# A four-layer graph network on one core: untransposed first weights, a table copy in pieces, larger rings, and layer 2's own rows added by an identity product

## What is computed

```
f0: w = relu(edge_attr @ W1.T + b1) @ W2.T + b2;  agg = segment_sum(w * x[src], dst)
    relu(x @ Ws.T + bs + agg @ Wn.T + bn)
f1: 10 times  out = 0.9 * segment_sum(w * out[col], row) + 0.1 * h;   out / theta
f2: 16 times  h = 0.9 * segment_sum(norm * h[row], col) + 0.1 * x     (self-loops added, norm from degrees)
f3: twice     h = prelu(segment_sum(norm * (h @ W)[src], dst) + b)    (self-loops added)
```

## Time and profile before

| | |
|---|---|
| runs (3) | 9433.23, 9444.26, 9446.84 us; median 9444.26 |
| profiled execution | 9456.96 us, its span 9455.1 us |
| busy: PE / PEld / DVE / ACT / POOL | 44% / 34% / 55% / 23% / 73% of the span |
| 0 to 323 us | histograms |
| 330 to 349 us | node_records |
| 355 to 988 us | rank_edges |
| 989 to 1318 us | prepare |
| 1323 to 4135 us | layer 1, 10 passes |
| 4135 to 8659 us | layer 2: own rows gathered and split until 4383, then 16 passes |
| 8659 to 9455 us | layer 3 |

### The profile page before, as it was taken

One profiled execution on the slowest core, in us unless ns is written; L12 is line 12 of the kernel. 1 busy time (PEld: TensorE's weight loads), 2 busy tenths in 40 slices (PEclk: granted clock), 3 DMA queues, 4 the chain that ended last, 5 costly groups with the idle time before them and its releaser, 6 DMA issues. The chain is left out here.

```text
span 9455.1 us, 78421 instructions
## 1 busy us (share of the span) xinstructions
PE 4182.3 (44%) x18929; PEld 3224.8 (34%) x18929; DVE 5165.0 (55%) x12775; ACT 2149.3 (23%) x5789; POOL 6906.2 (73%) x7074
## 2 busy tenths in 40 slices
PE   6566654444344443311444444444444443333643
PEld 5455542232222332211333333333333332223643
DVE  6566654454444445643555656555555665465454
ACT  1266542111011110331211111111111110036433
POOL 5565567777777777767777777777777777777777
PEclk9666665555555555555555555555555555555555
DMA  7755253333333333432444444433333343333311
GB/s 116 126 160 176 83 97 98 101 102 97 97 96 97 102 102 97 109 87 67 109 108 109 111 111 107 107 107 103 104 103 103 106 107 95 93 95 86 91 46 38
DMA packets 924098, 957.38 MB, mean 101 GB/s; under 512 B 385766, under 2 KB 814140, under 8 KB 923546
## 3 DMA queue, kind: packets, MB, share of 16 engines
q1 hardware_dynamic: 652470, 588.49, 20.8%
q0 software_dynamic: 225792, 323.35, 17.4%
q10 hardware_dynamic: 45382, 40.53, 1.3%
HBM read 561.02 MB, written 418.54 MB: 104 GB/s over the span
## 5 line engine op out<-in xcount | busy, mean ns | idle before, releaser
L1803 POOL DMA_INDIRECT l_g<-tab,l x2940 | 2889.3, 983 | 906.8 <-issue 852.7
L1972 DVE TENSOR_TENSOR_SCAN l_w<-l_m,l_w,bank 96x512 f32<-96x512 bf16 x1248 | 1591.9, 1276 | 2619.8 <-PE bank L1830 2613.1
L1830 PE MATMUL bank<-ident,l_g 128*96 128x128 f32 x5096 | 1334.0, 415 | 3309.6 <-DMA l_g<-tab,l 1706.0
L1830 PEld LDWEIGHTS bank<-ident,l_g 128*96 128x96 f32 x5096 | 843.3, 187 | 3905.8 <-DMA l_g<-tab,l 1877.3
L1803 POOL DMA_INDIRECT l_g<-tab,XM x1764 | 1731.0, 981 | 549.5 <-issue 514.9
L1841 PE MATMUL bank<-ident,l_w 96*128 96x96 f32 x5096 | 1055.3, 359 | 77.7 <-DVE l_w L1972 76.8
L1841 PEld LDWEIGHTS bank<-ident,l_w 96*128 96x128 f32 x5096 | 938.9, 227 | 121.0 <-DVE l_w L1972 108.3
L352 ACT ACTIVATE tail_sc<-tail_mv,eps_x 125x4 f32<-125x4 f32 (+1 forms) x149 | 44.3, 297 | 3511.5 <-DVE tail_mean L344 3416.0
L288 PE MATMUL bank<-tail_up,v 96*96 96x500 f32 (+1 forms) x298 | 296.4, 1098 | 437.5 <-DVE tail_up L279 437.5
L2016 DVE TENSOR_TENSOR l_o<-l_o,coef_d 128x384 f32<-128x384 f32 x735 | 411.9, 560 | 25.4
L2025 DVE TENSOR_TENSOR T<-l_o,XM 128x384 f32<-128x384 f32 x735 | 405.3, 555 | 0.0
(11 more groups left out here) (301 smaller groups left out, 9291.3 us busy)
## 6 DMA issues: line engine op xcount, KB each, us to landing
tab<-l_o SPq DMA_DIRECT2D x1176, 192.0 KB, 2.4
l_m<-mask_d SPq DMA_DIRECT2D x784, 96.0 KB, 2.7
l_m<-mask_s SPq DMA_DIRECT2D x490, 96.0 KB, 2.7
l_g<-tab,l POOLq DMA_INDIRECT x2940
l_g<-tab,XM POOLq DMA_INDIRECT x1764
x3t<-XM SPq DMA_DIRECT2D x98, 192.0 KB
x_meta<-in_x_dram SPq DMA_DIRECT2D x25, 750.0 KB
x1t<-XM ACTq DMA_DIRECT2D x100, 187.5 KB
```

The source lines that it names most:

```text
L1803: nc.gpsimd.indirect_dma_start(out=tile(G[q % RG], t), out_offset=None, in_=tables[0:table_at + (2 - p % 2) * TR, :] if p else first, in_o ...
L1830: last = nc.tensor.transpose(a_bank(q)[0:D, u:GE:U], G[q % RG][:, u * D:(u + 1) * D], self.ident[:, :])
L1972: v.tensor_tensor_scan(out=W[q % RW][:, :], data0=masks[q % RM][:, :], data1=a_bank(q)[0:D, :], initial=W[(q - 1) % RW][:, GE - 1:GE] if q ...
```

## The change

1. **First weights.** W1 and W2 are loaded as they lie in memory, into `w1_rows` (96 x 272) and `w2_rows` (96 x 96). PE turns them by five transposes into banks 4 and 5, and ACT copies them into `w1` and `w2`, ahead of its loop. POOL clears `w1_rows` in place of `w1`.
2. **Record tile.** It lies at column 8192 of XM and is cleared by POOL at the start of histograms, no more in node_records.
3. **rank_edges.** `lb` and `source_row` have semaphores of their own, `source_row` a ring of 3, `X` a ring of 10; loads run two groups ahead. The copy into `x_meta` is cut into 25 pieces, one a step for k = 4 to 28. The columns that the longer `X` takes in XM move two groups (8 gathers) from rank_edges to prepare: `BOTH_FIRST` 41 -> 39.
4. **Layer 2.** T holds the running value without XS. PE begins the bank by `ident x XS` (128x384) and adds the four back-turned tiles by ordinary products with the identity, no more by transposes. DVE adds T in place and scales T in place; SP stores from T; `update` and the ring O are gone there.

```
-                    for u in range(U):
-                        act.dma_start(w1[u * ED:(u + 1) * ED, u * D:(u + 1) * D], i["W1"].rearrange("c k -> k c")
+                        act.dma_start(w1_rows[:, u * (KU + ED):u * (KU + ED) + ED], i["W1"]).then_inc(first_weights, 16)
...
+                act.wait_ge(flipped, 2)
+                a_.activation(w1[:, :], self.bank[4][0:KU, 0:U * D], ACT.Copy).then_inc(set_, 1)
+                a_.activation(self.w2[0:D, :], self.bank[5][0:D, 0:D], ACT.Copy).then_inc(set_, 1)
...
+                def load_low(n):
+                    if n >= 2:
+                        sp.wait_ge(olts, 2 * (n - 1))
...
+                def load_sources(n):
+                    if n >= RS:
+                        sp.wait_ge(nears, (n - RS + 1) * U)
...
-                    if k % 2 == 0 and n < NI - 1:
-                        if n:
-                            sp.wait_ge(nears, n * U)
-                        load(n + 1)
+                    if k % 2 == 0 and n + 2 < NI:
+                        load_low(n + 2)
+                        load_sources(n + 2)
+                        load_snap(n + 2)
...
+                    if 4 <= k < 4 + MET:
+                        load_meta(k - 4)
...
+                def add_own(q):
+                    if q < NGP:
+                        pe.wait_ge(split, q + 1)
+                    if q >= RB:
+                        pe.wait_ge(summed.sem, summed.at + q - RB + 1)
+                    nc.tensor.matmul(b_bank(q)[:, 0:GD], self.ident[:, :], group(XS, q % NGP), start=True, stop=False,
+                                     skip_group_check=True)
...
+                    if smooth:
+                        for u in range(U):
+                            last = nc.tensor.matmul(b_bank(q)[:, u * D:(u + 1) * D], W[q % RW][:, u:GE:U],
+                                                    self.ident[0:D, 0:D], start=False, stop=True, skip_group_check=True)
...
-                    if smooth:
-                        v.tensor_tensor(out=there, in0=o, in1=group(XS, g), op=ALU.add).then_inc(ready.sem, 1)
```

More of the change, by code:

```diff
@@ L1685, in passes @@
             G = [tmp(f"g{r}", [P, GD]) for r in range(RG)]
-            O = [tmp(f"o{r}", [P, GD]) for r in range(RO)]
+            O = [tmp(f"o{r}", [P, GD]) for r in range(RO * power)]
             W = [tmp(f"w{r}", [D, GE]) for r in range(RW)]
@@ L1895, in weigh @@
                     for t in range(g * U, (g + 1) * U):
-                        to, of = (tile(Z[g % 2], t),) * 2 if conv else (tile(group(T, g), t), tile(O[q % RO], t))
-                        last = a.activation(to, of, ACT.Copy, scale=by[:, t:t + 1])
+                        x = tile(Z[g % 2] if conv else group(T, g), t)
+                        last = a.activation(x, x, ACT.Copy, scale=by[:, t:t + 1])
                     last.then_inc(kept.sem, 1)
@@ L2210, in passes @@
         made.at += {"power": K * NGP, "smooth": updates}.get(mode, 0)
-        ready.at += {"power": K * NGP, "smooth": updates}.get(mode, 0)
+        ready.at += K * NGP * power
         summed.at += 0 if power else K * NGP
```

118 lines of the change are left out of this document (65 added, 53 removed).

## The result

The changed kernel takes 9353.99 us (median of 4 runs, 9348.38 to 9368.66); the kernel before, in runs beside it, 9439.67 us (4 runs). The ratio is 0.9914, 95% interval 0.9898 to 0.993. That is 86 us less, where 218 were forecast: the sign is right, the size is not, and 9354 lies above the range of 9165 to 9320. The profiled execution's span is 9366.9 us.

The account below looks back on a forecast made before the run. POOL was taken to bound layer 2 and a DMA rank_edges. Terms -35.5 - 2.9 - 155 + 10 - 35 = -218 took the median from 9444.3 to 9226 us; own range 9175 to 9285, outer ends 9165 and 9320.

Parts of the forecast that it names:

- Part (a): rank_edges: the table copy, behind which SP's next load stood for 40.40 us, goes; 39 us if only this goes.
- Part (b): rank_edges: late source rows, all but 39 of DVE's 196 us of waiting, vanish with loads two groups ahead.
- The lower bound, -39: rank_edges: the least gain, 39 us, if only the hold behind the table copy goes; the most was 182.
- Rival A: rank_edges: transfers don't keep up, waits change place, half the gain goes (-80 instead of -155): 9301 us; chance 0.13.
- The lengthened gathers: Layer 2: without the update, POOL's gathers shorten; 60 us taken, bounds 0 and 80.
- The late pass edges and the phase: Between layer 2's passes: first gathers late, +14; scaling's phase against the gathers shifting with PE's lag, up to +10.
- Rival B: Layer 2: the update doesn't lengthen gathers, the scaling alone does; layer 2 at +14, kernel 9275 us; chance 0.09.
- Rival C: Layer 2: PE becomes the bound through back-turning and added products, 6.25 us a group, kernel 9886 us; chance 0.04.

Follow-up runs that it names:

- g2: Changed kernel with pieces issued by POOL and ring A of four, x3 stores cut to 96 numbers: 4.63 us a step in additions 6-30.
- g3: Changed kernel with pieces issued by POOL and ring A of four, x loads after the first ten cut to 96 numbers: 4.81 us a step, additions 6-30.
- h1: Changed kernel with 16-bit source rows, pieces issued by POOL and BOTH_FIRST 41: ratio 0.9934 to the kernel before, among stops.
- i1: Second run of the changed kernel with 16-bit source rows, pieces issued by POOL and BOTH_FIRST 41: ratio 0.9936 to the kernel before, among stops.
- j1: Third run, on another chip, of the changed kernel with 16-bit source rows, pieces issued by POOL and BOTH_FIRST 41: ratio 0.9935, among stops.
- f2: Changed kernel with the 25 pieces issued by POOL instead of SP, ring A still of three: 9349.57 us, ratio 0.991 to the kernel before.
- f0: The changed kernel itself, unedited, timed again as control: 9364.47 us, ratio 0.9919 to the kernel before.

## Why the prediction was right or wrong

1. **First weights, record tile: -35.5 and -2.9, measured -38.4 together.** POOL's first gather of rank_edges moves from 356.7 to 318.3. By place it is less exact: DVE's remainder came at 17.90, not 21.9, and histograms' last gather starts 39.6 us earlier; of this 1.2 us are given back by node_records, although DVE's copy there waits for PE and no more for POOL, as foreseen.

2. **rank_edges: -155, measured -14.7. This is the step that failed,** and in it the sentence that "the waits of now are of order and lead, since the share is only 0.60 while DVE idles". Part (a), the hold behind the table copy, did go: the lead-in is 39.5 us shorter. But the same 50,000 rows, in pieces, then took 35.0 us out of additions 6 to 30; the forecast had counted them as a risk and given them nothing of their own. Part (b), all but 39 of the 196 us of waits for source rows, was read as the price of loads issued late. It was the price of transfers that couldn't go faster. The waits went and others of the same sum took their place, and the 66 steps after the pieces gained 11.7 us, where their share of the forecast was 78 ((155 - 39) x 66 / 98). What the forecast did not do is ask what one step's 873 kB need: 190 GB/s of the two queues for a step of 4.6 us, where they had 144 to 152 in the stage before and no stretch of 20 us in that trace has over about 166. Nor is the share of 0.60 a reserve: it is the mean over 16 DMA engines, and two thirds of the bytes go over five of them. The lower bound, -39, was too good as well, since the copy only changed its form.

3. **Rival A** (the transfers don't keep up, the waits change their place) had the mechanism, ACT's landings and x among the names, at a chance of 0.13, and half the gain as its price; the measured kernel kept a tenth, so it lies above this rival's 9301 too. Its price should have been the bound itself.

4. **Eight gathers to prepare: +10, measured +9.8,** and DVE's wait for x_meta rows is 30.0 us as foreseen. The rest of prepare is 5 us longer; no run looked into it.

5. **Layer 2: -35, measured -41.3.** The lengthened gathers gave 45.0 us in the 15 passes (60 was taken, 0 and 80 were the bounds), at a mean of 0.967 (0.96 forecast), and the scatters 5.8. The late pass edges and the phase took less than the +24 set for them: all of POOL's idle time above its usual gap rose from 10.6 to 21.0 us in layer 2, 8.9 of these 10.4 ahead of the first gathers of passes. Both terms were too large and of opposite sign, so that the sum fits is in part luck. One reading behind the 60 was wrong: the instruction of 1.31 us is a scatter (L1760) and no gather. Gathers that start in the update have 1.107 us in the mean, scatters 1.159 where undisturbed ones have 0.977, so the direction held. PE's busy time in the passes, 2971 us, is under the 3300 forecast: the granted clock rose from 0.54 to 0.73 there. A group has 2971 / 735 = 4.04 us of PE in place of 4.5. The added product takes 1.19 us (1.4 forecast) and the back-turning 1.94 where the transposes had 0.82, so 1.1 more and not 0.8; what made the sum smaller is the rest, which the change left alone, at the higher clock: the turns fell from 1.04 to 0.87, the side job from 0.72 to 0.54. (The parts overlap, so they add up to more than the whole.)

6. **Rival B** (the update doesn't lengthen gathers) is refuted by the table above and by the 45 us. The Trainium skill (SBUF — State Buffer, Who interferes with whom), on which it drew, infers that such an operation does not hold up descriptor writing; these rows disagree, as far as the length of a gather shows it. **Rival C** (PE the bound, 9886 us): POOL waits for PE's steps 7.6 us in all of layer 2. Its point, 5.65 us of PE a group, is far from the 4.04 measured.

7. **Layer 1, -8.4,** wasn't forecast; its code is unchanged, and its gathers were 7.4 us shorter in all (1723.6 against 1731.0 us for 1764).

What stays open: no run gave the x transfers another number of rows, so that the five engines are the limit is read from the packets and from g2, g3, h1, i1 and j1, and not from a kernel that goes faster by it. The kernels with 192 kB less were only seen among stops, where the steps from 31 on say nothing. A ceiling of the queues themselves it is not: SP's single copy of x3d behind the stage of g2 runs at 331 GB/s from 1003 to 1053 us, with all 16 engines busy. And the runs do show that the ring of A, the place of the x3 store, the pieces and the order of SP's loads are not what sets the later steps.

## What to carry to other kernels

Before counting a wait for a transfer as lost by order, work out the traffic of one step and divide it by the step that is forecast: if no stretch of the trace reaches that rate, more lead may only move the wait to another name. A DMA share of 0.6 isn't a reserve of 0.4: it is a mean over 16 engines, so count over how many a transfer goes (here five for 125 rows, 16 for 128). An engine that is held at issuing a DMA shows as "issue" on its next instruction, so look at the lengths of its DMA issues. Under a POOL that never waits, each operation of DVE with both inputs in SBUF has a price (0.1 us and more for a gather that starts in it), and folding one into a PSUM accumulation on PE was worth 41 us here, where PE had room.

## What was not expected of the hardware

- The two queues of SP and ACT together kept to 144 to 147 GB/s in the later part of the stage and 152 to 160 in the part before it (in the changed kernels that is the part behind the pieces), in kernels with quite different waits, while the share of busy DMA engines stood at 0.51 to 0.59.
- A plain transfer of 125 rows goes over five DMA engines and one of 128 rows over 16, by the number of its 4-byte packets and by the packets in flight (at most 9 against 21).
- A transfer of 2000 rows of 32 bytes holds SP's next load 4.19 to 6.70 us at its issue in the rows shown; issued by POOL it costs 1.08 us of POOL, and the stage of f2 is 16 us shorter than f0's.
- TensorE's granted clock in layer 2's passes was 0.54 before, nearly all of it the 1.2 GHz level, and is 0.73 now, with a good part at 2.4 GHz; PE was busy 1678 of 3971 us before and 2971 of 3966 now.
- The same kernel takes 9.4 ms at one time and 11.0 ms at another, with nearly equal lengths of single instructions and stops of many engines at once between them; the cause was not found.
